# Four layers on one core: where eight of the scatters and one batch's logits stand around the start of the first mixture of experts

## The chip, the cores and the metric

The program runs on one core of a Trainium2 chip. Four layers, each an attention and a mixture or feed-forward part, are one launch. The metric is the device time of that launch in microseconds (us). The engines that matter here are TensorE (PE), VectorE (DVE), ScalarE (ACT), GpSimd (POOL), which also issues the indirect DMAs, and SyncE (SP), which issues the plain ones.

## The reference

The input is x of 8 x 256 tokens with 256 channels. The change lies between the attention and the mixture of the first layer, so only that is shown. What the attention computes does not matter for the change beyond that it handles the 8 sequences one after the other.

```python
x = x + _L0_attn_ref(_layernorm(x), ...)          # causal, 16 heads of 16
x = x + _L0_ffn_ref(_layernorm(x), ...)

def _L0_ffn_ref(x, w_gate, w_shared_up, w_shared_down, w_up, w_down):
    TOPK, CAP, E = 6, 128, 64
    x_flat = x.reshape(-1, C)                      # 2048 tokens
    y_s, g_s = jnp.split(x_flat @ w_shared_up, 2, axis=-1)
    shared = jax.nn.silu(g_s) * y_s @ w_shared_down
    scores = jax.nn.sigmoid(x_flat @ w_gate)
    _, topk_idx = jax.lax.top_k(scores, TOPK)
    w = ...                                        # the six scores, made to sum to 1
    # place of a token in its expert's list: how many earlier tokens chose that expert
    x_disp = zeros((E, CAP, C)).at[flat_e, pos].set(x_flat[token_ids], mode='drop')
    h_r = silu(g_r) * v_r                          # up product of each expert, split in two
    out_r = jnp.einsum('ech,ehd->ecd', h_r, w_down)
    routed = (y_ts.reshape(N, TOPK, C) * w[:, :, None]).sum(axis=1)
    return shared + routed
```

## The kernel before

**Stages.** Each stage is a block of its own (`with nc.Block()`), with one instruction stream for each engine. A block ends with a drain of each engine and a barrier, then POOL clears the stage's semaphores, then comes a second barrier (class `Stage`, lines 64 and 65). So an instruction of the mixture's stage starts only when all engines have ended the attention's. The attention's block is opened in line 1103, the mixture's in line 1813.

**Batches and quads.** The 2048 tokens are 16 tiles of 128, and a batch is one sequence, thus two tiles (QT = 2). The attention runs 32 quads (`QUADS`), four for each batch. The routing of a batch for the mixture is woven into the quads that come after its attention: class `Places`, with the steps statistics, normalised rows, transposes ("turned"), logits and choice, ranks, gates, and sending. `EARLY = 6`: batches 0 to 5 are routed in the quads, batches 6 and 7 at the start of the mixture's stage.

**Scatters.** A routed token is sent to its six experts. For one tile and one of the six choices, POOL issues one indirect DMA that writes 128 rows of 336 floats to the table `places` in HBM (`send`, line 1540). That is 12 scatters for a batch and 96 in all. Batches 0 to 4 are sent by `pool_end` in the quads, three scatters a quad. Batch 5 gets its gates in the last quad, and `pool_end` sends the first `in_front` of its 12 scatters there, behind POOL's four small operations (`rstd`) for batch 6. They are the last instructions of POOL in the attention. The rest of batch 5 is sent by POOL's program of the mixture's stage, which first runs `rstd` for batch 7, then sends what is left of batch 5, then waits for the gates of batch 6 (`row_ready`) and sends its 12, and the same for batch 7. One semaphore, `places.sent`, counts all 96.

**The loop over the experts.** SP waits for all 96 scatters and then loads the row tile of one expert after another (line 1823). PE transposes it, multiplies it up, transposes the hidden tile and multiplies it down, ACT and DVE do the activation, the product and the copies, and POOL adds the product to the sums with an indirect DMA (line 2020). Nothing of the loop can start before the last scatter has landed.

**PE at the start of the mixture's stage.** With `first` = batch 6 and `second` = batch 7, PE runs in the order written in the program: `turn(first)` (four transposes of the normalised rows into bank 4, line 1572), `shared_up(0)` (the shared expert's up products of the first 512 tokens, 8 instructions in the trace, line 1842), `logits(first)` (line 1579), `turn(second)`, `ranks(first)` (lines 1586 and 1587), `logits(second)`, and then the rest of the shared expert. `logits` waits until ACT has copied the transposes of its batch (`places.copied`, line 1906). `shared_up(0)` waits for the copies of batches 0 and 1, which were made in the attention. DVE takes the logits of batch 6 through `read_logits`, `pick` and `choose`, then PE makes the ranks, and DVE goes on with `read_ranks`, `place`, `weigh` and `gates` (the last, line 1712, writes the gates into the rows and releases POOL).

Of the kernel before, what the change touches and what calls it, by code (L numbers as in the profile page):

```python
# [43 lines left out]
def need(eng, sem, value):  # L44

    if isinstance(value, int) and value <= 0:
        return
    eng.wait_ge(sem, value)
# [1407 lines left out]
class Places:  # L1456
# [4 lines left out]
    FIRST, PER_BATCH, EARLY = 7, 4, 6  # L1461
    STATS, NORMED, TURNED, CHOSEN, RANKED, GATED, SENT = 0, 1, 2, 2, 3, 4, 5
    SETUP = 7
    in_front = 4

    def __init__(self, core, cfg, scratch, stack, router_in, earlier_in, base_in, token_in, shared_in):
        nc, E = core.nc, cfg.E
# [280 lines left out]
def fixed_experts_stage(core, cfg, places, up_in, down_in):  # L1748
# [15 lines left out]
    def steps_of(enter, up, turn, leave):  # L1764

        for n in range(E + 3):
            for work, at in ((enter, n), (up, n - 1), (turn, n - 2), (leave, n - 3)):
                if work and 0 <= at < E:
                    work(at)
# [13 lines left out]
    def logits_of(b):  # L1783
        return route_bank[b][:, 0:QT * E]

    def ranks_of(b):
        return route_bank[b][:, 256:256 + QT * E]

    with Stage(core) as st:
# [23 lines left out]
        with nc.Block() as block:  # L1813

            @block.sync
            def _(sp):
                sp.dma_start(up_w[:], up_in).then_inc(weights_loaded, 16)
                sp.dma_start(down_w[:], down_in).then_inc(weights_loaded, 16)
                sp.wait_ge(places.sent, 16 * TILES * TOP)
                for e in range(E):  # L1820
                    if e >= RING:
                        sp.wait_ge(added[(e - RING) % SUMS], landed(e - RING))
                    sp.dma_start(tile_rows[e % RING][:], scratch.rows[e * ROOM:e * ROOM + P, :]).then_inc(row_loaded[e % RING], 16)
                for r in range(SUMS):
                    sp.wait_ge(added[r], landed(E - SUMS + r))
                    for n in range(PARTS):
                        sp.dma_start(part_of(results[r], n), part_of(scratch.sums[r][0:TILES * P, :].rearrange("(p t) c -> p t c", p=P), n))\
                            .then_inc(results_loaded[r][n], 16)

            @block.tensor  # L1830
            def _(pe):
                def turn(b):
                    places.transposes(pe, b, [turn_bank[b][:, n * P:(n + 1) * P] for n in range(QT * KT)]).then_inc(places.turned, 1)

                def shared_up(c):
                    tokens = slice(c * CHUNK, (c + 1) * CHUNK)
                    pe.wait_ge(places.copied, (c + 1) * (B // CHUNKS))
                    need(pe, shared_added, 2 * (c - 1))
                    for u, (to, done) in enumerate(zip(shared_bank[c % 2], (s_gate_done, s_up_done))):
                        for kt in range(KT):  # L1840
                            at = (u * KT + kt) * SH
                            ins = nc.tensor.matmul(to[0:SH, :], shared[:, at:at + SH], norm_t[:, kt, tokens], start=(kt == 0), stop=(kt == KT - 1))
                        ins.then_inc(done, 1)

                def shared_down(c):
                    pe.wait_ge(s_hidden_ready, c + 1)
                    for j in range(TC // 2):
                        for t in (2 * j, 2 * j + 1):
                            ins = nc.tensor.matmul(shared_bank[c % 2][j][:, (t % 2) * C:(t % 2 + 1) * C], s_hidden[c % 2][:, t * P:(t + 1) * P],
                                                   shared[0:SH, 2 * KT * SH:2 * KT * SH + C], start=True, stop=True)  # L1850
                        ins.then_inc(s_y_done, 1)

                def transpose_rows(e):
                    pe.wait_ge(row_loaded[e % RING], 16 * (e // RING + 1))
                    need(pe, x_t_copied, e - 1)
                    for kt in range(KT):
                        ins = nc.tensor.transpose(x_bank[e % 2][:, kt * P:(kt + 1) * P], tile_rows[e % RING][:, kt * P:(kt + 1) * P], core.ident[:])
                    ins.then_inc(x_t_done, 1)

                def up(e):  # L1860
                    if e == 0:
                        pe.wait_ge(shared_added, 2 * CHUNKS)
                        pe.wait_ge(weights_loaded, 32)
                    pe.wait_ge(x_t_copied, e + 1)
                    need(pe, hidden_ready, e)
                    for kt in range(KT):
                        ins = nc.tensor.matmul(up_bank[:, 0:2 * H], x_t[e % 2][:, kt, :], up_w[:, e, kt, :], start=(kt == 0), stop=(kt == KT - 1))
                    ins.then_inc(up_done, 1)

                def transpose_hidden(e):  # L1870
                    if e == 0:
                        pe.wait_ge(zeroed, 1)
                    pe.wait_ge(hidden_ready, e + 1)
                    need(pe, h_copied, e)
                    nc.tensor.transpose(h_bank[:, 0:P], hidden[e % 2][:], core.ident[:]).then_inc(h_done, 1)

                def down(e):
                    pe.wait_ge(h_copied, e + 1)
                    need(pe, product_ready, e - 1)
                    at = slice(e % PACK * H, e % PACK * H + H)  # L1880
                    nc.tensor.matmul(y_bank[e % 2][:, 0:C], hidden_t[e % 2][at, :], down_w[at, e // PACK, :], start=True, stop=True).then_inc(y_done, 1)

                first, second = LAST
                pe.wait_ge(places.loaded, 16 * len(places.early_loads))
                turn(first)
                shared_up(0)
                places.logits(pe, first, logits_of(first))
                turn(second)
                places.ranks(pe, first, ranks_of(first))
                places.logits(pe, second, logits_of(second))  # L1890
                shared_up(1)
                shared_down(0)
                places.ranks(pe, second, ranks_of(second))
                shared_up(2)
                shared_down(1)
                shared_up(3)
                shared_down(2)
                shared_down(3)
                steps_of(transpose_rows, up, transpose_hidden, down)
# [1909 lines left out]
```

## Time and profile before

| what | us |
|---|---|
| median of 3 runs | 2983.94 |
| their range | 2980.67 to 2985.32 |
| the profiled execution, its own time | 2979.16 |
| span of the profiled execution | 2977.4 |
| granted TensorE clock, mean over the span | 0.921 |
| the attention's last instructions end (PE, POOL, DVE) | 249.4, 248.9, 250.1 |
| first instruction of the mixture's stage (SP) | 255.07 |
| last of the 96 scatters ends | 299.62 |
| first load of the loop over the experts | 301.23 |

Times in the rows count from the start of the span. The profiled execution took 1.76 us more than its span. It is shorter than each of the three timed runs; the four together average 2982.3.

In a timeline a row is: start, length, engine, line, operation, output and input tiles, how many were merged, and in brackets how long the engine had been idle and what ended that. PEld is PE's weight load. A name with a q (POOLq, DVEq) is the sequencer of the engine, which runs drains and semaphore instructions. These are in the trace, but don't count as busy time. The granted clock (PEclk) is 0.50 at 1.2 GHz and 1.00 at 2.4 GHz.

### The profile page before, as it was taken

Reading aid. Unit: us, or ns where it says so; the run is one execution under the profiler, and the core shown is the slowest. Engines: PE = TensorE matmul, PEld = TensorE weight load, DVE = VectorE, ACT = ScalarE, POOL = GpSimd, SP = SyncE. Lnnn points to the kernel's source line nnn. Section 1 sums busy time; section 2 is a strip of 40 time slices with the busy share of each in tenths; the row PEclk is TensorE's granted clock in tenths of the full one; section 3 lists DMA queues with packets and bytes.
Section 4 is the critical chain, followed back from the end, with each engine's and each line's share of the span. In section 5 each row is a group of like instructions: output and inputs, shape, how many; then the busy total and the mean of one; then the engine's idle time right before and its main releaser. Section 6 shows DMA issues by size and latency. Waiting matters only on the chain. (4 is left out here: it accounts for less than half of the span.)

```text
span 2977.4 us, 64818 instructions
## 1 busy us (share of the span) xinstructions
PE 2598.9 (87%) x19777; PEld 2191.0 (74%) x19777; DVE 1950.5 (66%) x6166; ACT 1522.3 (51%) x4590; POOL 950.7 (32%) x884
## 2 busy tenths in 40 slices
PE   6886995899986799999967499999999998799996
PEld 4663663666654699999946389999999988467774
DVE  5785334777875788788853567777777788344554
ACT  5872222899985555555553344444444444123332
POOL 3366453211003322222225411111111155436664
PEclk8998555999998899999989799999999999899998
DMA  8324565999201201010024433333333233846677
GB/s 293 88 85 190 111 113 137 346 371 346 78 2 46 78 29 54 30 61 29 29 96 154 158 103 102 92 96 102 102 95 93 86 131 132 331 102 114 116 117 160
DMA packets 260129, 371.94 MB, mean 125 GB/s; under 512 B 32112, under 2 KB 226088, under 8 KB 256912
## 3 DMA queue, kind: packets, MB, share of 16 engines
q1 hardware_dynamic: 219344, 301.42, 31.6%
q0 software_dynamic: 40512, 67.14, 11.1%
q8 instruction: 139, 2.28, 0.3%
q14 instruction: 134, 1.10, 0.1%
HBM read 109.03 MB, written 175.55 MB: 96 GB/s over the span
## 5 line engine op out<-in xcount | busy, mean ns | idle before, releaser
L671 PE MATMUL bank<-norm_t_high,w 128*128 128x256 f32 (+1 forms) x2176 | 446.9, 287 | 8.5 <-DVE w L870 8.5
L835 ACT ACTIVATE probs<-bank,neg_max 128x256 f32<-128x256 f32 (+1 forms) x512 | 224.5, 443 | 404.0 <-DVE inv L951 395.8
L1279 ACT ACTIVATE probs<-neg_scores,bound 128x256 f32<-128x256 f32 (+1 forms) x768 | 367.2, 486 | 23.5 <-DVE bound L1358 22.5
L671 PEld LDWEIGHTS bank<-norm_t_high,w 128*128 128x128 f32 x2176 | 363.4, 194 | 9.1 <-issue 9.1
L671 PE MATMUL bank<-norm_t_low,w 128*128 128x256 f32 (+1 forms) x1088 | 310.2, 285 | 0.0
L1358 DVE CUSTOM_DVE_ANT_0 neg_scores<-bank,table 128x256 f32<-128x256 f32 (+1 forms) x768 | 262.2, 396 | 52.3 <-PE bank L1189 52.3
L986 POOL TENSOR_TENSOR summed<-turned 128x512 f32<-128x512 f32 x64 | 82.4, 1288 | 612.8 <-DVE turned L902 603.0
L3269 POOL DMA_INDIRECT sums<-norm_ffn x127 | 197.3, 1553 | 156.1 <-ACT norm_ffn L3166 120.6
L731 PE MATMUL bank<-k,q 128*128 128x256 f32 (+1 forms) x1536 | 245.2, 296 | 0.0
L957 DVE SCALAR_TENSOR_TENSOR x_sb<-bank,inv,x_sb 128x256 f32<-128x256 f32 (+1 forms) x512 | 224.3, 480 | 29.3 <-DVE inv L951 19.2
L843 ACT ACTIVATE probs_t<-bank 128x384 fp32r<-128x384 f32 (+1 forms) x256 | 139.4, 545 | 202.5 <-PE bank L741 202.3
L671 PE MATMUL bank<-w,out_t 128*128 128x256 f32 x1536 | 229.1, 285 | 10.2 <-DVE out_t L943 10.2
L758 PE MATMUL bank<-probs_t,v 128*128 128x256 f32 (+1 forms) x1536 | 218.2, 278 | 3.3 <-issue 2.2
L671 PEld LDWEIGHTS bank<-w,out_t 128*128 128x128 f32 x1536 | 201.6, 190 | 13.9 <-DVE out_t L943 11.5
L671 PEld LDWEIGHTS bank<-norm_t_low,w 128*128 128x128 f32 x1088 | 211.0, 194 | 0.0
L1203 PE MATMUL bank<-ident_sb,probs 128*128 128x128 f32 x1408 | 194.8, 279 | 15.6 <-ACT probs_t L1286 15.6
L731 PEld LDWEIGHTS bank<-k,q 128*128 128x128 f32 x1536 | 197.2, 191 | 10.2 <-issue 0.2
L758 PEld LDWEIGHTS bank<-probs_t,v 128*128 128x128 f32 x1536 | 199.4, 190 | 5.3 <-DVE probs_t L938 2.4
L1203 PEld LDWEIGHTS bank<-ident_sb,probs 128*128 128x128 f32 x1408 | 155.4, 142 | 60.8 <-issue 30.7
L3118 PE MATMUL bank<-weights,shared 128*128 x508 | 174.5, 467 | 0.7 <-DVE shared L3228 0.3
L1403 POOL TENSOR_SCALAR k_placed<-k_t,place 128x512 f32<-128x512 f32 x48 | 74.4, 1565 | 305.4 <-ACT k_t L1253 305.4
L938 DVE TENSOR_TENSOR probs_t<-bank,probs_t 128x384 fp32r<-128x384 f32 (+1 forms) x256 | 158.2, 618 | 16.2 <-ACT probs_t L843 14.9
(426 smaller groups left out, 6003.0 us busy)
## 6 DMA issues: line engine op xcount, KB each, us to landing
rows<-blank SPq DMA_DIRECT2D x1, 77976.0 KB, 241.4
z<-norm_t_high SPq DMA_DIRECT2D x96, 256.0 KB, 2.5
z<-norm_t_low SPq DMA_DIRECT2D x96, 256.0 KB, 2.5
norm_ffn<-rows SPq DMA_DIRECT2D x127, 152.0 KB, 2.6
weights<-in_experts SPq DMA_DIRECT2D x1, 17024.0 KB, 49.9
q_turned<-halves SPq DMA_DIRECT2D x256, 64.0 KB, 2.0
k_turned<-halves SPq DMA_DIRECT2D x256, 64.0 KB, 2.0
places<-blank_wide SPq DMA_DIRECT2D x1, 10752.0 KB, 33.2
```

The lines of the kernel that those rows point to most:

```text
L671: ins = nc.tensor.matmul(out, stationary(a), moving(c), start=(kt == 0 and m == 0), stop=(kt == n - 1 and m == 2))
L731: ins = nc.tensor.matmul(s[:, score_columns(causal, t)], qq[a][:, j, t * P:(t + 1) * P], kk[c][:, kj, 0:width], start=False, stop=(n == 2 ...
L758: ins = nc.tensor.matmul(o_bank[:, to], vv[a][:, kt, jv * P:(jv + 1) * P], pp[c][:, of], start=(kt == 0 and n == 0), stop=(kt == QT - 1 an ...
L835: ins = nc.scalar.activation(probs[j % 2][:, t, 0:width], s_bank[j % 2][:, score_columns(causal, t)], ACT.Exp, bias=neg_max[j % 2][:, t:t ...
L843: nc.scalar.activation(probs_t[j % 2][0][:], t_bank[:, 0:NB], ACT.Copy).then_inc(t_high, 1)
L938: nc.vector.tensor_tensor(probs_t[j % 2][1][:], t_bank[:, 0:NB], probs_t[j % 2][0][:].bitcast(F32), ALU.subtract).then_inc(t_low, 1)
L957: ins = nc.vector.scalar_tensor_tensor(tile, y_bank[j % 2][:, t * C:(t + 1) * C], inv[j % 2][:, t:t + 1], tile, ALU.mult, ALU.add)
L1203: ins = nc.tensor.transpose(t_bank[g % 2][:, at:at + P], probs[q % 2][g][:, t, kt * P:(kt + 1) * P], core.ident[:])
L1279: ins = nc.scalar.activation(probs[q % 2][g][:, t, 0:width], neg_scores[g][:, t, 0:width], ACT.Exp, bias=bound[q % 2][:, g, t:t + 1], scal ...
L1358: ins = nc.vector.tensor_tensor_reduce(out=neg_scores[g][:, t, 0:width], in0=s_bank[g][:, t * S:t * S + width], in1=table[:, at:at + width ...
L3118: ins = nc.tensor.matmul(up_bank[e % 2][:, 0:COLUMNS], x_t[e % 2][:, kt, :], weights[:, kt * COLUMNS:][:, bass.ds(expert[e], COLUMNS)], st ...
L3269: nc.gpsimd.indirect_dma_start(scratch.results[e % SUMS], bass.IndirectOffsetOnAxis(ids, 0), product[e % OUT_RING], None, compute_op=ALU.a ...
```

## The change

Two edits, both around the border between the attention's block and the mixture's. `in_front` goes from 4 to 8: POOL issues eight scatters of batch 5 behind its last `rstd` in the attention, and four fewer in the mixture's stage. And on PE, `logits(first)` stands in front of `shared_up(0)` rather than behind it.

```diff
 class Places:
     FIRST, PER_BATCH, EARLY = 7, 4, 6
     STATS, NORMED, TURNED, CHOSEN, RANKED, GATED, SENT = 0, 1, 2, 2, 3, 4, 5
     SETUP = 7
-    in_front = 4
+    in_front = 8
...
                 turn(first)
+                places.logits(pe, first, logits_of(first))
                 shared_up(0)
-                places.logits(pe, first, logits_of(first))
                 turn(second)
                 places.ranks(pe, first, ranks_of(first))
                 places.logits(pe, second, logits_of(second))
```

On PE, at the start of the mixture's stage: `bank4<-ident_sb,rows_9` is `turn(first)`, `bank2<-router_w_11,norm_ffn_8` is `logits(first)`, the two rows into bank 0 and bank 1 are `shared_up(0)`, `bank5` is `turn(second)`, and the last row begins `ranks(first)`. The order counts a matmul once where the trace has two records of it.

```order
 L1572 MATMUL bank4<-ident_sb,rows_9 128x128 x4
+L1579 MATMUL bank2<-router_w_11,norm_ffn_8 128x64 x4
 L1842 MATMUL bank0<-norm_ffn_8,shared_10 64x512 x2
 L1842 MATMUL bank1<-norm_ffn_8,shared_10 64x512 x2
-L1579 MATMUL bank2<-router_w_11,norm_ffn_8 128x64 x4
 L1572 MATMUL bank5<-ident_sb,rows_9 128x128 x4
 L1586 MATMUL bank2<-chosen_bf_18,earlier_bf_15 128x128
```

The four matmuls of the logits have moved up past the four of the shared product, and nothing else on PE moved.

On POOL, at the end of the attention's block (the branch of line 1103 leaves it, the instruction of line 64 is the clearing of the semaphores):

```order
 L1533 TENSOR_TENSOR shift<-meanvar,rstd 128x2
 L1535 TENSOR_SCALAR shift<-shift 128x2
-L1540 DMA places_0<-rows_9,slot_28 131072x336 x4
+L1540 DMA places_0<-rows_9,slot_28 131072x336 x8
 L1103 UNCONDITIONAL_BRANCH
 L64 ISA
```

Four more scatters now stand ahead of the block's end. In the mixture's stage 28 follow the `rstd` of batch 7, where 32 did; the instructions of DVE, ACT and SP are the same in both programs.

## Rows read from the trace of the kernel before

**Rows 1.** The page: the span, and the chain that ended last.

```profile
span 2977.4 us, 64818 instructions
PE bank L3118 5%; PE bank L3135 4%; PE bank L3107 1%; PE bank L3126 1%; PE bank L3084 1%; PE bank L3095 1%; DMA rows<-rows,slot 1%; DMA weights<-sums 0%; DMA shared<-in_shared 0%; DMA sums<-norm_ffn 0%; DMA norm_ffn<-rows 0%; DVE x_sb L3258
```

**Rows 2.** Line 1103 (attention's end), 248 to 258 us: ns min/median/max, first and last start.

```profile
L1103 POOLq DRAIN  x1: 10563/10563/10563, 243.7 to 243.7; - x1
L1103 PEldq DRAIN  x1: 3337/3337/3337, 246.1 to 246.1; - x1
L1103 DVEq DRAIN  x1: 723/723/723, 249.4 to 249.4; - x1
```

**Rows 3.** Timeline of POOL around the border of the two stages.

```profile
247.97 0.96 POOL L1540 DMA_INDIRECT places<-rows,slot  x1 [0.30 <-issue]
...
258.04 1.07 POOL L1540 DMA_INDIRECT places<-rows,slot  x1 [0.17 <-issue]
...
269.58 0.96 POOL L1540 DMA_INDIRECT places<-rows,slot  x1 [1.53 <-DVE rows L1712]
...
298.66 0.96 POOL L1540 DMA_INDIRECT places<-rows,slot  x1 [0.30 <-issue]
```

**Rows 4.** The same drain of POOL at the ends of two other stages.

```profile
L611 POOLq DRAIN  x1: 12966/12966/12966, 2530.5 to 2530.5; - x1
L1103 POOLq DRAIN  x1: 6296/6296/6296, 823.8 to 823.8; - x1
```

**Rows 5.** Timeline of POOL: its last instruction in those two stages.

```profile
2537.10 0.96 POOL L2771 DMA_INDIRECT rows<-rows,slot  x1 [0.30 <-issue]
823.81 6.18 POOL L1403 TENSOR_SCALAR k_placed<-k_t,place 128x512 f32<-128x512 f32 x4 [38.02 <-ACT k_t L1253]
```

**Rows 6.** Stretches of the span: length, busy us by engine, PEclk, DMA share, GB/s.

```profile
250.00:254.00 4.00, 0.00 (x0) 0.00 (x0) 0.11 (x1) 0.00 (x0) 0.00 (x0) 0.93 0.00 0
...
259.00:260.00 1.00, 1.00 (x3) 0.36 (x2) 0.00 (x0) 0.00 (x0) 0.69 (x2) 0.50 1.23 524
260.00:261.00 1.00, 1.00 (x3) 0.27 (x2) 0.00 (x0) 0.00 (x0) 0.70 (x2) 0.87 1.22 524
```

**Rows 7.** Timeline of all engines from the start of the mixture's stage.

```profile
255.27 1.09 PE L1572 MATMUL bank<-ident_sb,rows 128*128 128x128 f32 x4 [5.88 <-PEq L65]
256.29 5.60 PE L1842 MATMUL bank<-norm_ffn,shared 128*64 128x512 f32 x8
256.39 0.60 ACT L1906 ACTIVATE norm_ffn<-bank 128x512 f32<-128x512 f32 x1 [11.37 <-PE bank L1572]
...
258.90 0.23 PEld L1842 LDWEIGHTS bank<-norm_ffn,shared 128*64 128x64 f32 x1 [0.63 <-issue]
259.76 0.23 PEld L1842 LDWEIGHTS bank<-norm_ffn,shared 128*64 128x64 f32 x1 [0.63 <-issue]
260.44 0.14 PEld L1842 LDWEIGHTS bank<-norm_ffn,shared 128*64 128x64 f32 x1 [0.45 <-issue]
260.87 0.14 PEld L1842 LDWEIGHTS bank<-norm_ffn,shared 128*64 128x64 f32 x1 [0.29 <-issue]
261.82 1.10 PE L1579 MATMUL bank<-router_w,norm_ffn 128*128 128x64 f32 x8
262.76 0.61 PE L1572 MATMUL bank<-ident_sb,rows 128*128 128x128 f32 x4
262.96 0.29 DVE L1654 COPY padded<-bank 128x128 f32<-128x128 f32 x1 [6.53 <-PE bank L1579]
265.47 0.23 PE L1586 MATMUL bank<-chosen_bf,earlier_bf 128*128 128x128 bf16 x1 [2.10 <-DVE seen L1675]
...
269.01 0.29 DVE L1712 TENSOR_TENSOR rows<-exps,inv 128x128 f32<-128x128 f32 x1
```

**Rows 8.** Timeline of DVE and of SP's queue, up to the loop.

```profile
295.91 0.69 DVE L1950 TENSOR_TENSOR x_sb<-bank,x_sb 128x512 f32<-128x512 f32 x1 [0.17 <-PE bank L1849]
301.23 96.34 SPq L1823 DMA_DIRECT2D tile_rows<-places  x39
```

## The prediction

> **What bounds the kernel now.** The page gives the size of the whole [rows 1]; its chain of what ended last is followed back through the last layer only, so it says nothing of the first mixture, where the change lies. There I read the timeline at both sides of the border between attention and mixture, and the records of the sequencers.
>
> The mixture's side first. The loop over the experts starts when the last of the 96 scatters has landed. POOL issues them one behind the other: from 269.58 to 298.66 there are 24, so one takes (298.66 - 269.58) / 23 = 1.264 us, of which 0.96 is in the record [rows 3]. SP's first load follows at 301.23 [rows 8]. The shared product is done before that: DVE's last addition starts at 295.91 and takes 0.69, which ends 3.0 us ahead of the last scatter (298.66 + 0.96 = 299.62) [rows 3, 8]. So POOL's scatters are the path. They were held up once in this stage: POOL waited 1.53 us until DVE had written the gates of batch 6, and went on at 269.58 [rows 3]. At this place the two things that the change touches meet. Behind it stand the 24 scatters of batches 6 and 7, and the change leaves them as they are. The time is therefore start of the stage + way to the gates of batch 6 + 24 scatters.
>
> Then the attention's side. PE's drain ends at 246.1 + 3.34 = 249.4 and DVE's at 249.4 + 0.72 = 250.1, but POOL's began at 243.7 and lasted 10.56, until 254.26 [rows 2]. POOL's last scatter had ended at 247.97 + 0.96 = 248.93 [rows 3]. The drain held 5.33 us longer, and it is what ended the block: PE's first instruction of the next stage starts at 255.27 [rows 7]. A look at POOL's busy time alone would call it free from 248.93 on and put the end at DVE's 250.1. The drain says that it is the last.
>
> **The change part by part.**
>
> Four more scatters in the attention. They stand behind the last `rstd`, directly ahead of the drain. 4 x 1.264 = 5.06 us, so the last ends at 253.99. The question is what the drain then does. At the end of the last layer's attention, six scatters end at 2537.10 + 0.96 = 2538.06 and the drain at 2530.5 + 12.97 = 2543.47, thus 5.41 later; where POOL's last work is no DMA, it ends at 823.81 + 6.18 = 829.99 and the drain at 823.8 + 6.30 = 830.10, thus 0.1 later [rows 4, 5]. So 5.3 to 5.4 us is a price that follows the last scatter, be it behind four or six of them, and not a fixed point of time. The block then ends at 254.26 + 5.06. The cover that hid nothing before hides nothing now. I take +5.06 for the start of the mixture's stage, with 0 below (if the 5.33 us are slack in which four scatters fit). All engines start later by that.
>
> Four fewer scatters in the mixture's stage. POOL starts its first one 258.04 - 255.27 = 2.77 behind PE's start [rows 3, 7]. It now has 4 rather than 8 to issue before batch 6 and is free at (on the old clock of the stage) 258.04 + 4 x 1.264 = 263.1. That would be worth 5.06 if nothing else came. But the gates of batch 6 were ready only at 269.01 + 0.29 = 269.30 [rows 7], after all eight scatters. The saving is swallowed by the wait: with the gates unmoved POOL still goes on at 269.58, and the wait grows from 1.53 by the time of four scatters, to 6.6 us. Worth 0, except as far as the gates come earlier.
>
> Logits ahead of the shared product. This is what moves the gates. On the old clock of the stage: the transposes end at 256.36, the copy on ACT ends at 256.39 + 0.60 = 256.99 [rows 7], and the logits can start at some 257.03; PE is idle 0.7 us there, where before it went straight into the shared product, which does not need this copy. The logits took 1.10 us at the high clock [rows 7]; now they run at 1.2 GHz, since the granted clock was 0.50 in 259 to 260 and rose within 260 to 261 [rows 6]. The transposes took 1.09 at the low clock and 0.61 at the high one [rows 7], a factor of 1.8, so I take 2.0 us for the logits (between 1.1 and 2.2): they end at 259.0. DVE needed from 262.96 to 265.47 for read, pick and choose, 2.51 us [rows 7], and is ready for the ranks at 261.6. But PE is not. Between them stand now `shared_up(0)` and `turn(second)`. An instruction of the shared product took 259.76 - 258.90 = 0.86 at the low clock and 260.87 - 260.44 = 0.43 at the high one [rows 7]. The 0.87 of 260 to 261 puts the rise at 260.26 [rows 6]. From 259.0 to there 1.5 of the 8 are done, the other 6.5 take 2.8, until 263.1, and the transposes 0.6, until 263.7. So the ranks start at 263.7 rather than 265.47: 1.8 us earlier, bounded by PE and no longer by DVE. The gates follow by the same DVE work, 1.8 earlier. Logits at the high clock's pace give 2.2; a rise 1.7 later gives about 0.9.
>
> PE's side afterwards: the wait for the ranks is gone, so the rest of the shared product comes no later within the stage. It starts 5.06 later in all, and what waits for the last addition would see it at 296.6 + 5.1 = 301.7 at most, while PE's first work of the loop comes after SP's first load at 301.2 + 3.3 = 304.5 [rows 8]. Covered, with 2.8 us left. SP's loads of the experts' weights (6.3 MB by the tiles' sizes) also start with the block, 5.06 later; at the 524 GB/s of 259 to 260 [rows 6] they take some 12 us, and are in place 30 us before the loop.
>
> The sum: 5.06 (the block ends later) + 0 (four fewer, swallowed) - 1.8 (gates of batch 6 earlier) = +3.3 us. Nothing behind it is changed: 24 scatters, landing, loop, three layers. Of the profiled execution that makes 2979.16 + 3.3 = 2982.5. That execution is faster than each of the timed runs; the four average 2982.3, which gives 2985.6, and the median gives 2987.2. I take **2986**, which is +0.11%, inside the 0.2% (6.0 us) that a measurement of this kernel can tell from no change.
>
> A rule of the skill, against a row. In the trace no DMA moves any byte from 250 to 254, while the drain still holds [rows 6]. By the Trainium skill, DMA: Bandwidth & Descriptors, section "Anatomy of one DMA — SWDGE (gpsimd) path", a DMA issued by GpSimd has a fixed cost of about 2.0 us plus bytes over 436 GB/s. If the drain waited for just that, the estimate from this page for one scatter (128 rows of 336 floats, 0.17 MB) would be 2.4 us, and the drain would have ended at 251.3; the row has 254.26, so the measurement decides. The four scatters would by that page end the new block at 256.4, +2.1 rather than +5.06.
>
> **The rivals.**
>
> B, the drain's time is slack. If the 5.33 us behind the last scatter run out from something earlier than that scatter, some of the four fit in. At the far end the stage starts where it did and only the swap counts: 0 - 1.8 = -1.8 us, 2980.5 by the average; halfway (2.5 - 1.8) it is +0.7, 2983. For it: DMA traffic had ended by 250 and PE and DVE too, so nothing visible is worked on [rows 2, 6]. Against it: the tail was the same in two stages of quite different ends, and nearly nothing without scatters [rows 4, 5]. The rule of the Trainium skill above would put it at 2.1 - 1.8 = +0.3, near the middle of this case.
>
> C, the swap brings nothing. The order on PE changes, but the gates don't come earlier, since PE's idle 0.7 us and the logits at 1.2 GHz eat it, or since the ranks are held by something that I don't see. Then the full +5.06 stays: 2987.4 by the average. For it: PE's rows say that it is busy without a gap from 256.29 to 263.4 [rows 7], and the swap adds work at the low clock to that. Against it: 2.1 us of idle on PE ahead of the ranks is there to be taken [rows 7]. This is also the case in which the change doesn't do what it says.
>
> D, slower. The mechanism is the clock at `shared_up(0)`, which now stands between the logits and the ranks. PE starts after 11 us of idle, rather than 5.9, and has a new gap of 0.7 us in its first 2 us. If the clock then stays at 1.2 GHz until the shared product is through, that takes 8 x 0.86 = 6.9, from 259.2 to 266.1, and the transposes 1.1: the ranks start at 267.2 rather than 265.47, and the gates are 1.7 later rather than 1.8 earlier. 5.06 + 1.7 = +6.8, 2989.1 by the average, +0.23%. It decides from the point where the rise comes later than some 264 on the old clock, 3.7 us behind that of before (then the ranks are where they were). Against it: PE is busy from 257.03 on nearly without a break.
>
> **How the numbers follow.** Forecast (+2.5 to +4.3): 0.61. B: 0.14, about half of it around its middle. C: 0.13. D: 0.08. The rest, 0.04, is for what I don't see, on either side. Timed runs differ by some 2 us each way, so the forecast and C reach beyond 6 us now and then, C more often: slower by over 0.2% is D's larger part (0.06), from C 0.05, from the forecast 0.05 and of the rest 0.02, which makes 0.18. Faster by over 0.2% needs -6: B at its end with the runs against it, 0.03, and 0.02 of the rest, 0.05. Within 0.2% remains 0.77. The range: below it reaches into B (2980.5) and above to D (2989) with 2 to 3 us for the runs, 2980 to 2992.
>
> **What would show it.** In the changed kernel's trace: eight scatters behind `rstd` in the attention, the last ending at some 254.0. The drain of POOL in line 1103 ending at 259.3 (B: before 258), and PE's first instruction of the stage at 260.3. Logits from 262.1 to 264.1, the ranks at 268.8 (C: 270.5; D: 272.3). POOL's wait for the gates of batch 6 at 4.8 us rather than 1.53, and the 24 scatters from 272.9 at 1.264 each. SP's first load at 304.5. Wrong would be the forecast if the drain's tail shrinks as scatters are added, if the rise of the clock falls elsewhere by over 2 us, or if the stages behind the loop move against each other.

## The result

The changed kernel takes 2990.41 us (median of 11 runs) against 2985.32 for the kernel before (also 11, measured beside it). Two of the 11 before were slow ones (3352.30 and 4206.07 us) and are left out of the ratio, so it is not that of the two medians. The ratio is 1.0025, with a 95% interval of 1.0013 to 1.0036: slower by some 7.5 us, between 3.9 and 10.7. The forecast was +3.3 us, inside the 0.2% that can't be told from no change. The time lies in the range, but the measured ratio is above the 0.2% that was called most likely, though its interval begins below it.

The profiled execution of the changed kernel has a span of 2995.9, 18.5 more than before. That is no measure of the change: at 2997.73 us it is the second longest of its kernel's 11 runs, and of the 18.5 us 2.7 had come about ahead of the first changed instruction and 10.2 behind the loop's first load, in code that is the same. The two profiles are therefore compared over one **stretch**, from the start of POOL's last `rstd` operation in the attention (line 1535, the last instruction ahead of the scatters in front) to SP's first load of the loop over the experts (line 1823). All that the change touches lies in it. Before it is 301.23 - 243.71 = 57.5 us, after it 309.54 - 246.37 = 63.2, thus +5.65.

Timeline of POOL in the changed kernel (start, length, engine, line, operation, tiles, idle time before and what ended it); it answers to [rows 3]:

```profile
246.37 0.19 POOL L1535 TENSOR_SCALAR shift<-shift 128x2 f32<-128x2 f32 x1
246.73 1.07 POOL L1540 DMA_INDIRECT places<-rows,slot  x1 [0.17 <-issue]
...
255.70 0.96 POOL L1540 DMA_INDIRECT places<-rows,slot  x1 [0.30 <-issue]
...
270.01 0.96 POOL L1540 DMA_INDIRECT places<-rows,slot  x1 [0.30 <-issue]
277.83 0.96 POOL L1540 DMA_INDIRECT places<-rows,slot  x1 [6.86 <-DVE rows L1712]
...
306.97 0.96 POOL L1540 DMA_INDIRECT places<-rows,slot  x1 [0.30 <-issue]
```

The drains at the end of its attention (ns min/median/max, first and last start), which answer to [rows 2]:

```profile
L1103 POOLq DRAIN  x1: 15958/15958/15958, 246.3 to 246.3; - x1
L1103 DVEq DRAIN  x1: 725/725/725, 252.2 to 252.2; - x1
```

The timeline of SP's queue, which answers to [rows 8]:

```profile
263.14 0.34 SPq L1817 DMA_DIRECT2D up_w<-in_up  x1
...
309.54 20.01 SPq L1823 DMA_DIRECT2D tile_rows<-places  x11
```

POOL's eighth scatter ends at 256.66, DVE is done at 252.9, and POOL's drain holds the block until 246.3 + 15.96 = 262.3. In the mixture's stage POOL sends its four, then waits 6.86 us for the gates of batch 6, where it had waited 1.53.

All engines from the start of the mixture's stage, which answers to [rows 7]:

```profile
263.33 1.09 PE L1572 MATMUL bank<-ident_sb,rows 128*128 128x128 f32 x4 [11.16 <-PEq L65]
264.46 0.60 ACT L1906 ACTIVATE norm_ffn<-bank 128x512 f32<-128x512 f32 x1 [16.77 <-PE bank L1572]
265.11 1.97 PE L1579 MATMUL bank<-router_w,norm_ffn 128*128 128x64 f32 x8 [0.69 <-ACT norm_ffn L1906]
...
267.00 6.30 PE L1842 MATMUL bank<-norm_ffn,shared 128*64 128x512 f32 x8
267.11 0.29 DVE L1654 COPY padded<-bank 128x128 f32<-128x128 f32 x1 [2.62 <-PE bank L1579]
...
269.09 0.49 DVE L1675 TENSOR_TENSOR seen<-seen,chosen 128x64 bf16<-128x64 bf16 x2
...
273.24 0.66 PE L1572 MATMUL bank<-ident_sb,rows 128*128 128x128 f32 x4
...
273.73 0.22 PE L1586 MATMUL bank<-chosen_bf,earlier_bf 128*128 128x128 bf16 x1
```

And the granted clock there (stretch, its length, busy us of PE, PEld, DVE, ACT and POOL, the clock, DMA share and GB/s), which answers to [rows 6]:

```profile
271.00:272.00 1.00, 1.00 (x2) 0.23 (x1) 0.00 (x0) 0.00 (x0) 0.00 (x0) 0.50 1.37 589
272.00:273.00 1.00, 1.00 (x3) 0.23 (x1) 0.00 (x0) 0.00 (x0) 0.00 (x0) 0.81 1.36 578
```

DVE has the choice of batch 6 ready at 269.6. PE gets to the ranks at 273.73, since `shared_up(0)` stands between and runs at 1.2 GHz until 272.4. So the 5.65 us are made up as follows, each taken as a difference of two starts. The mixture's stage starts (SP, line 1817) 16.77 us behind the last `rstd` operation rather than 11.36: +5.41. From there POOL's first scatter of batch 6 comes after 14.69 us rather than 14.51: +0.18. The 24 scatters and the landing take 0.06 more.

### The profile page after: what moved, and what is told of

The parts are those of the page before. It is cut to its first block and busy times, and to the rows that moved or that the text cites. A ratio compares the mean times of both kernels' runs of the same rounds, so it can differ in the third digit from the quotient of the medians.

```text
span 2995.9 us, 64818 instructions
## 1 busy us (share of the span) xinstructions
PE 2607.7 (87%) x19777; PEld 2197.6 (73%) x19777; DVE 1949.8 (65%) x6166; ACT 1524.1 (51%) x4590; POOL 952.5 (32%) x884
## 5 line engine op out<-in xcount | busy, mean ns | idle before, releaser
L1279 ACT ACTIVATE probs<-neg_scores,bound 128x256 f32<-128x256 f32 (+1 forms) x768 | 366.9, 485 | 24.5 <-DVE bound L1358 23.6
L1358 DVE CUSTOM_DVE_ANT_0 neg_scores<-bank,table 128x256 f32<-128x256 f32 (+1 forms) x768 | 262.0, 396 | 56.7 <-PE bank L1189 56.7
```

The source lines that it names most:

```text
L1279: ins = nc.scalar.activation(probs[q % 2][g][:, t, 0:width], neg_scores[g][:, t, 0:width], ACT.Exp, bias=bound[q % 2][:, g, t:t + 1], scal ...
L1358: ins = nc.vector.tensor_tensor_reduce(out=neg_scores[g][:, t, 0:width], in0=s_bank[g][:, t * S:t * S + width], in1=table[:, at:at + width ...
```

## The experiments

Two theories were open. **T**: each scatter in front of the drain costs its time in full, since POOL's drain ends the block a fixed time behind POOL's last instruction. **K**: the swap's gain is real but is lost in the shared product, which PE runs at the low clock. Their rivals: that the swap itself did the harm, that the drain's time can hold other work, and that the late clock was chance.

The table has for each run: scatters in front; POOL's drain, from the end of POOL's last operation; start of the mixture's stage from the start of the last `rstd` operation; rise of the clock to 2.4 GHz and start of the ranks of batch 6, both from PE's first instruction of the stage (the rise read from stretches of a quarter us); the stretch; and, where it was timed, the ratio to the kernel before with its interval. "High" means that the stage began at the high clock and fell from it or kept it. The drain's start stands in the lines to a tenth of a us; the table takes it to the hundredth from the traces, and so differs by up to 0.05 from the 4.95, 5.33 and 5.60 of the expectations.

| run | in front | drain | stage start | rise | ranks | stretch | ratio |
|---|---|---|---|---|---|---|---|
| before | 4 | 5.30 | 11.36 | 5.0 | 10.20 | 57.5 | |
| changed | 8 | 5.63 | 16.77 | 9.1 | 10.40 | 63.2 | 1.0025 (1.0013 to 1.0036) |
| e1_scatters_only | 8 | 5.63 | 16.76 | 6.1 | 10.78 | 63.5 | 1.0020 (1.0008 to 1.0032) |
| e2_swap_only | 4 | 5.31 | 11.37 | 7.8 | 9.77 | 57.1 | 1.0000 (0.9987 to 1.0012) |
| e3_front0 | 0 | 4.99 | 7.11 | high | 7.93 | 57.0 | 1.0007 (0.9996 to 1.0018) |
| e4_front12 | 12 | 5.96 | 22.15 | 4.3 | 9.83 | 68.7 | |
| e5_swap_front6 | 6 | 5.47 | 14.08 | 6.7 | 9.23 | 59.3 | |
| e6_pe_kept_busy | 8 | 5.63 | 16.74 | high, fell | 9.31 | 62.0 | 1.0019 (1.0003 to 1.0035) |
| e7_front2 | 2 | 5.14 | 8.68 | high, fell | 9.43 | 56.7 | 1.0004 (0.9989 to 1.0018) |
| e8_narrow_ahead | 4 | 5.30 | 11.38 | 8.9 | 13.83 | 61.2 | |
| e9_shared_behind | 8 | 5.63 | 16.75 | 12.0 | 6.30 | 59.1 | 1.0011 (1.0002 to 1.0020) |
| e10_ahead_of_rstd | 2 | 5.14 | 8.67 | high, fell | 9.65 | 55.2 | 1.0002 (0.9990 to 1.0014) |
| e11_memsets_behind | 4 | 5.32 | 15.38 | 3.7 | 9.54 | 61.1 | |
| e12_before_again | 4 | 5.30 | 11.37 | 5.5 | 10.49 | 57.9 | 1.0001 (0.9986 to 1.0016) |

The runs e5 to e8, e11 and e12 were made on chips on which the kernel before takes 3068 to 3070 us rather than 2983 to 2985; each ratio is to the kernel before on the same chip.

**One edit at a time.** e1 and e2 take the two edits apart.

```diff
-    in_front = 4
+    in_front = 8
```

> Only in_front 8, the order on PE as before. I measure the stretch from POOL's last rstd operation in the attention (line 1535) to SP's first load of the loop (line 1823): 57.5 us before, 63.1 in the changed kernel. Theory (a scatter ahead of the drain costs its full time, the drain ends 5.3 to 5.6 us behind the last one, and the wait for the gates swallows what is saved later): block end 5.1 to 5.3 later within the stretch, stretch 62.6 to 62.9, and POOL waits some 6.6 us for the gates of batch 6. Rival (the swap is what costs, the scatters fit in partly): stretch 60 or less. Timed: about +5 us, ratio 1.0017.

```diff
                 turn(first)
+                places.logits(pe, first, logits_of(first))
                 shared_up(0)
-                places.logits(pe, first, logits_of(first))
```

> Only the swap on PE, in_front 4 as before. Theory (the swap gains up to 1.8 us when the clock rises as in the kernel before, and nothing or a little loss when it rises late; which of the two is chance): stretch between 55.7 and 57.7, ranks 8.4 to 10.4 us behind PE's start of the stage (10.2 before, 10.4 in the changed kernel). Rival (the swap always delays the rise of the clock): rise about 8.9 us behind PE's start as in the changed kernel, ranks at 10.4, stretch 57.7. Timed: within 0.1% of before.

The scatters alone give a stretch of 63.5 and a ratio of 1.0020, the swap alone 57.1 and 1.0000. The loss is that of the scatters. With the swap alone the stretch is 0.4 us shorter than before (57.5; 57.9 in e12), with a rise of the clock at 7.8. Theory and rival of e2 both allowed for such a stretch, so e2 doesn't decide between them; e5 and e8 below bear on it. What I expected of e1 held but for 0.6 us: POOL's wait was 7.25 rather than 6.6, with the ranks at 10.78.

**How many scatters.** e3, e4, e5 and e7 change only the number: the diff is that of e3, and e4 has 12 in its place, e7 has 2, and e5 is the changed kernel, with the swap, and 6.

```diff
-    in_front = 4
+    in_front = 0
```

> in_front 0, the order on PE as before: no scatter stands behind the last rstd. Theory (the drain ends 5.3 us behind the last scatter, whatever stands between): POOL's last scatter is that of the last quad, so the drain ends before DVE is through, the block ends by DVE and the mixture's stage starts some 4 us earlier; POOL then has 12 scatters ahead of the gates of batch 6 and is the later one, so of the 4 us only about 0.5 is left: stretch 57.0. Rival (the drain's 5.3 us are paid at the block's end whatever POOL did last): block end 5.3 us behind the last rstd operation, no earlier start than 1.3 to 3 us, stretch 58 to 60.

> in_front 12, the order on PE as before: all of batch 5 ahead of the drain. Theory: linear, 8 x 1.264 = 10.1 us later than before, drain's end again 5.3 to 5.6 behind the last scatter, POOL waits some 11.6 us for the gates of batch 6, stretch 67.6 to 68.1. Rival (the time behind the last scatter grows with each scatter, as 5.33 with four and 5.60 with eight may be read): 5.9 or more with twelve, stretch 68.2 or more.

> in_front 2, the order on PE as before. Theory: the stage starts at 11.36 - 2 x 1.35 = 8.7 behind the last rstd operation, POOL is bound by its own scatters (ten of batch 5 in the stage, the gates are ready before they are through), stretch 55.9 to 56.3, 1.2 to 1.6 us under the kernel before. Rival (the drain has a fixed part that shows with any scatter behind rstd): start at 10 or later, stretch 57.5. Timed: within 0.1% of before, too little to be told by the clock of the device; the stretch decides.

The start of the stage is at 8.7, 11.4, 14.1, 16.8 and 22.2 for 2, 4, 6, 8 and 12: 1.35 us for each, of which 1.265 is the scatter and 0.083 a longer drain. With none it is 7.1, and there the block ended by DVE: POOL's drain ended at 249.0, DVE's at 250.1. Here the expectation was wrong in one point. Drains of e3, the second one that of DVE:

```profile
L1103 POOLq DRAIN  x1: 5060/5060/5060, 243.9 to 243.9; - x1
L1103 DVEq DRAIN  x1: 725/725/725, 249.4 to 249.4; - x1
```

POOL's last scatter had ended at 242.25 and its last `rstd` operation at 244.01. The drain did not end 5.3 behind the scatter but 6.75, which is 4.99 behind the `rstd` operation. e11 below is about that. The stretch of e3, 57.0, came as expected: 4.25 us earlier start, and POOL with its 12 scatters of batch 5 then later than the gates. e4 shows the other end. Its drain of POOL:

```profile
L1103 POOLq DRAIN  x1: 21065/21065/21065, 243.8 to 243.8; - x1
```

And POOL's wait for the gates of batch 6 in e4, in the timeline:

```profile
280.34 1.07 POOL L1540 DMA_INDIRECT places<-rows,slot  x1 [11.59 <-DVE rows L1712]
```

With no scatter of batch 5 left in the stage, POOL waits 11.59 us there, and the stretch is 68.7, above the 67.6 to 68.1 of the theory and at what the rival said: the time behind the last scatter does grow, by 0.083 us for each scatter, to 5.96. e7 was 0.4 us longer than expected. One of its scatters started 1.76 us behind the one before rather than 1.27, which is all of it; I have no cause for that.

**What the drain waits for.** e11 puts other work behind the scatters.

```diff
                     dispatch.pool_end(pool, q, ...)
+                for n in range(4):
+                    pool.wait_ge(zeroed, 2 + n)
+                    nc.gpsimd.memset(windows[0][:].rearrange("p t h w -> p (t h w)"), 0.0).then_inc(zeroed, 1)
```

> The kernel before (in_front 4), with four memsets of a tile that nobody reads any more behind POOL's last scatter of the attention, 0.95 us each and some 4 us in all. Theory S (the 5.3 us of the drain run from the last scatter on, whatever POOL does in them): the memsets fit in, drain's end 5.3 to 5.5 behind the last scatter, start of the stage 11.4 to 11.6 behind the last rstd operation, stretch as before. Rival O (the drain pays about 5 us behind POOL's last operation once scatters have gone ahead; for it speaks that with in_front 0 the drain ended 4.95 behind the last rstd operation and 6.71 behind the last scatter): drain's end 9 us or more behind the last scatter, start at 15 or later, stretch 61 or more. In between (7 to 8 us behind the last scatter) would say that a part of it runs on beside other work.

Timeline of POOL in e11, and then its drain:

```profile
272.80 0.96 POOL L1543 DMA_INDIRECT places<-rows,slot  x1 [0.30 <-issue]
273.76 3.99 POOL L1421 MEMSET windows<- 128x1024 f32 x4
```

```profile
L1103 POOLq DRAIN  x1: 6288/6288/6288, 276.8 to 276.8; - x1
```

The memsets end at 277.75 and the drain at 283.07: 5.32 behind the memsets, 9.31 behind the last scatter. The rival O was right: the drain's time runs from POOL's last instruction, whatever that is.

This is not the completion of the scatters. SP's first load waits for all 96 of them, and in all fourteen traces it starts 1.6 us behind the end of the last one's record (before: 299.62 and 301.23), while in e11 the drain ended 9.31 us behind the last scatter. By the Trainium skill, DMA: Bandwidth & Descriptors, section "Anatomy of one DMA — SWDGE (gpsimd) path", a DMA issued by GpSimd has a fixed cost of about 2.0 us. The trace is near that: the load comes 2.57 us behind the start of the last scatter.

The traces also show what sets the length. The attention's block has 60 scatters of batches 0 to 4 and those in front, and the drain ends 4.99, 5.14, 5.30, 5.47, 5.63 and 5.96 us behind POOL's last instruction with 60, 62, 64, 66, 68 and 72 of them: 0.083 us for each indirect DMA of the whole block. Two other blocks of the kernel before bear this out. The last layer's attention has 66 and 5.46 us (the prediction's 5.41, which was read from tenths) [rows 4, 5]. The block of line 2234 has 32 + 47 = 79; the last of them ends at 1663.35, POOL's last addition at 1680.43 and the drain at 1686.97, thus 6.54 behind the addition, again 0.083 for each, although no indirect DMA had been issued for 23.6 us. POOL there (the groups with counts, two rows of the timeline, and the drain):

```profile
L2594 POOL DMA_INDIRECT products<-shared,norm_t x47 | 45.1, 959 | 36.1 <-ACT shared L2405 35.5 <-issue 0.6
L2587 POOL DMA_INDIRECT rows<-token_rows,slot x32 | 30.9, 965 | 33.6 <-ACT token_rows L2375 24.2 <-issue 9.4
```

```profile
1662.39 0.96 POOL L2594 DMA_INDIRECT products<-shared,norm_t  x1 [0.30 <-issue]
...
1671.97 8.46 POOL L2600 TENSOR_TENSOR x_sb<-x_sb,weights 128x1024 f32<-128x1024 f32 x3 [0.63 <-DMA weights<-products]
```

```profile
L2234 POOLq DRAIN  x1: 10041/10041/10041, 1676.9 to 1676.9; - x1
```

In a block without indirect DMAs the drain ends 0.1 behind the last instruction [rows 4, 5]. The count does not give the length in the two blocks with a loop over experts, whose last indirect DMAs add to the sums: 96 with 6.6 us and 157 with 3.8. So the 0.083 is read from these three blocks, and no run set out to test it. What the drain does in this time the traces don't say.

**The clock.** e5 is one more case with the swap, and e8 takes the gap on PE and the late shared product apart.

> The changed kernel with in_front 6. So far the mixture's stage starts 7.1, 11.4, 16.8 and 22.2 us behind POOL's last rstd operation with 0, 4, 8 and 12 scatters in front. Theory (each one costs 1.35 us, of which 1.264 is its own): start at 14.1. And on the clock, theory A (it rises 3.2 to 5.4 us behind the first instruction of the shared product, which the swap puts 3.7 rather than 1.0 behind PE's start): rise 6.9 to 9.1 behind PE's start, ranks at 9.3 to 10.4, stretch to SP's first load 59.8 to 60.7. Rival (the late rise in the two kernels with the swap is chance): a rise as in those without it, 4.2 to 6.2, ranks at 8.0 to 9.0, stretch down to 58.4.

```diff
                 turn(first)
+                for _ in range(2):        # batch 5's logits, into a part of a bank that is overwritten later
+                    for t in range(QT):
+                        for kt in range(KT):
+                            nc.tensor.matmul(route_bank[second][:, t * E:(t + 1) * E], ...)
                 shared_up(0)
```

> The kernel before, but PE makes batch 5's logits twice more, into a part of a bank that is overwritten later, between the transposes of batch 6 and the shared product. So the narrow matmuls stand ahead of the shared product as in the changed kernel, but PE has no gap in front of them. Added work: 16 records of 0.24 us, 3.8 us on PE. Theory A (what counts is how late the shared product starts): first shared instruction 4.8 us behind PE's start, rise 8.0 to 10.2 behind PE's start. Rival G (it is the gap of 0.7 us that put the rise off): rise 4.2 to 6.2 behind PE's start as in the kernels without the swap. Stretch longer than 57.5 by 2 to 4 us in either case, from the added work.

PE in e8 from the start of the stage, and then the stretch in which its clock rises:

```profile
277.85 1.09 PE L1572 MATMUL bank<-ident_sb,rows 128*128 128x128 f32 x4 [4.68 <-PEq L65]
278.73 3.52 PE L1889 MATMUL bank<-router_w,norm_ffn 128*128 128x64 f32 x16
282.17 5.93 PE L1842 MATMUL bank<-norm_ffn,shared 128*64 128x512 f32 x8
```

```profile
286.00:287.00 1.00, 1.00 (x2) 0.23 (x1) 0.00 (x0) 0.00 (x0) 0.76 (x1) 0.60 0.15 65
```

PE is busy without a gap from 277.85 on, and the clock was granted in full only from 286.8 on, 8.9 behind PE's start but 4.6 behind the first instruction of the shared product. So it is not the gap of 0.7 us. Over the ten kernels of the table in which PE starts the stage at the low clock the rise comes 3.7 to 12.0 us behind PE's start, but 2.7 to 5.4 behind the start of `shared_up(0)` (before: 255.27 + 4.98 - 256.29 = 4.0, after: 263.33 + 9.05 - 267.00 = 5.4). e5 lies at 3.0, just below the 3.2 that I had given as the lower end; its ranks (9.23) and stretch (59.3) also lie just under what theory A gave and above what its rival gave. The swap puts the start of the shared product from 1.0 to 3.7 behind PE's start, and the rise goes with it. With the swap the ranks then come at 10.40, 9.77 and 9.23, without it at 10.20, 10.78, 9.83, 10.49 and 9.54: on the mean 9.80 against 10.17. That is 0.4 us in favour of the swap, but cases of the same order differ by over 1 us by where the rise falls, so that it can't be told from nothing.

**Giving PE the high clock, or nothing to run between.** e6 keeps PE busy over POOL's drain; e9 moves the shared product away.

```diff
                 for kind in ("inv", "spread", "y"):
                     product(kind, B - 1)
+                if dispatch:
+                    pe.wait_ge(bound_ready, 4 * QUADS)
+                    for n in range(9):        # nobody reads the result
+                        nc.tensor.matmul(s_bank[0][:], out_t[:, 0, 0:P], wo[:]..., start=True, stop=True)
```

> The changed kernel, and at the end of PE's program in the attention nine matmuls of 512 columns whose result nobody reads; they run while POOL still sends and drains, so that PE comes to the mixture's stage without the long idle time. Theory (the swap's gain was lost to the low clock): the clock is high when the stage starts, the ranks come 6.5 to 7 us behind PE's start rather than 10.4, POOL's wait for the gates shrinks from 6.9 to some 3.3, and the stretch from 63.2 to some 59.5; the start of the stage stays at 16.8 behind the last rstd operation, since PE is done before POOL. Rival (the clock has no part in it, or the ranks wait for something else on PE): ranks at 9.5 or later, stretch 62 or more. Timed: some 3.5 us less than the changed kernel, still 2 us over the kernel before.

```diff
                 places.logits(pe, first, logits_of(first))
-                shared_up(0)
                 turn(second)
                 places.ranks(pe, first, ranks_of(first))
+                shared_up(0)
                 places.logits(pe, second, logits_of(second))
```

> The changed kernel (in_front 8, logits of batch 6 first), and shared_up(0) moved on behind the ranks of batch 6, so that nothing of the shared product stands between that batch's logits and its ranks. Theory (the swap's gain is lost in the shared product, which PE runs at the low clock while DVE's choice is ready): the ranks start about 6.3 us behind PE's start, when DVE is ready, rather than 10.4; POOL's wait for the gates shrinks from 6.9 to some 2.5; its 24 scatters start 10.5 us behind the stage's start, stretch 58.7 to 59.3, start of the stage unmoved at 16.8. Rival (the ranks wait for something else, DVE or the transposes of batch 7): ranks at 9 or later, stretch 62 or more. Timed: some 4 us less than the changed kernel, still 1 to 2 over the kernel before.

e6 missed. Its granted clock over the start of the stage:

```profile
285.00:286.00 1.00, 0.00 (x0) 0.00 (x0) 0.00 (x0) 0.00 (x0) 0.00 (x0) 1.00 0.00 0
286.00:287.00 1.00, 0.56 (x4) 0.46 (x4) 0.71 (x2) 0.00 (x0) 0.00 (x0) 0.87 0.00 0
287.00:288.00 1.00, 0.31 (x3) 0.05 (x1) 0.57 (x5) 0.60 (x1) 0.42 (x2) 0.50 1.56 459
...
293.00:294.00 1.00, 1.00 (x3) 0.36 (x2) 0.00 (x0) 0.00 (x0) 0.90 (x1) 0.72 0.15 66
```

The stage began at the high clock, but PE had been idle from 284.34 to 286.44, and the clock fell at 286.7 and was back at 293.6. The ranks came at 9.31, where 6.5 to 7 was expected. So e6 settles nothing about what a high clock would give to the swapped order, and no other run does. For the old order e3 has it: the clock was high from PE's start until behind the ranks, and these came at 7.93 rather than 10.20. e9 does settle what stands in the way of the ranks. PE in e9:

```profile
265.99 1.11 PE L1572 MATMUL bank<-ident_sb,rows 128*128 128x128 f32 x4
...
268.51 0.29 PE L1586 MATMUL bank<-chosen_bf,earlier_bf 128*128 128x128 bf16 x1 [1.41 <-DVE seen L1675]
...
268.84 6.28 PE L1842 MATMUL bank<-norm_ffn,shared 128*64 128x512 f32 x8
```

The ranks come at 6.30, when DVE is ready, POOL's wait shrinks from 6.86 to 2.90 (2.5 was expected) and the stretch from 63.2 to 59.1, as expected. It is still 1.6 us over the kernel before (ratio 1.0011), since the start of the stage is where eight scatters put it.

**A shorter row of scatters.** By T few scatters in front are best, and POOL's own row is then the path. e10 also fills POOL's wait for DVE's statistics.

```diff
-    in_front = 4
+    in_front = 2
...
+                ahead = 2
+                for n in range(places.in_front, places.in_front + ahead):
+                    places.send(pool, places.EARLY - 1, n)
                 places.rstd(pool, B - 1)
                 for b in range(places.EARLY - 1, B):
                     pool.wait_ge(places.row_ready, b + 1)
-                    for n in range(places.in_front if b == places.EARLY - 1 else 0, QT * TOP):
+                    for n in range(places.in_front + ahead if b == places.EARLY - 1 else 0, QT * TOP):
```

> in_front 2, the order on PE as before, and in the mixture's stage POOL sends two scatters of batch 5 ahead of the rstd of batch 7, in the time in which it waits for DVE's statistics. Theory (POOL's row of scatters is the path from the stage's start on, so 1.2 us of its idle time go): start of the stage 8.7 behind the last rstd operation, no wait for gates, last scatter's start 44.1 to 44.3 behind the stage's start rather than 45.4, stretch 55.3 to 55.6, about 2 us under the kernel before. Rival (batch 7's rows come later by the later rstd, and hold PE and thereby the ranks of batch 6 up): POOL waits for the gates, stretch 57 or more. Timed: 0.05 to 0.1% under the kernel before, which five rounds will hardly tell from nothing.

The stretch is 55.2, 2.3 under the kernel before and a little better than expected, and POOL waits for no gates. The ratio of 1.0002 (0.9990 to 1.0014) can't tell 2 us from nothing, so this is no proven gain for the whole.

**The control.**

> The kernel before once more, unchanged, as a control: it gives a second profile of it with its own state of the clock, and says what a ratio of 1 looks like. Theory: ratio 1.000 with an interval of 0.0012 to either side, rise of the clock 4.2 to 6.2 behind PE's start, ranks at 9.8 to 10.8, stretch 57.2 to 58.0. Were the ratio 1.0005, the 1 to 2 us by which most timed ratios of this study exceed what the stretch shows would be an offset of the comparison; were the stretch 59 or more, the one profile of before would have been a lucky one.

The kernel before against itself gives 1.0001 (0.9986 to 1.0016), and its second profile a stretch of 57.9. So the profile of before was an ordinary one. The timed differences of this study are by 0 to 3 us larger than those of the stretches (7.5 against 5.65 for the changed kernel). Their intervals hold the smaller numbers in each case, and the control gives no offset; whether something behind the loop has a part in it stays open.

## Why the prediction was wrong

The larger term and its sign were right: the drain had been seen as what ends the block, and the four scatters as not hidden. +5.06 was forecast for the start of the stage, +5.41 measured; the 0.35 more is the drain's own growth (4 x 0.083 = 0.33). That it is a price "that follows the last scatter", the same "be it behind four or six of them", was wrong: e11 shows that it follows POOL's last instruction of any kind, and it grows with all the scatters of the block. The two tails that I compared stand behind 64 and 66 scatters, not four and six. For this change that was worth only the 0.33. Rival B, that the drain's time is slack, fell: neither scatters nor memsets fitted into it.

Four fewer scatters in the stage were costed at 0, since the wait for the gates would swallow them; the wait grew to 6.86, where 6.6 stood for unmoved gates. Right.

The step that failed is the swap, the term of -1.8. It measured +0.18 in the profiled kernel, and -0.4, within the scatter of the cases, by the mean of the ranks over three with it and five without. Its first half held: the logits took 1.97 us where 2.0 was taken, DVE was ready for the ranks 6.2 us behind PE's start (269.58 - 263.33), where 6.3 was forecast. What failed is "the 0.87 of 260 to 261 puts the rise at 260.26": I took the time of the rise from the order before and left it standing on the clock of the stage, 5.0 us behind PE's start. It goes with the shared product, which the swap itself had put off by 2.7 us. At 9.05 instead of 4.98, more than six of the eight records (272.38 - 267.00 over 0.86 us) ran at the low pace before the ranks, rather than the 1.5 of the sum. The text had the point from which it turns, "later than some 264 on the old clock" or 8.7 behind PE's start; the rise at 9.05 was just past it, and the swap gave just nothing. With the rise as measured the prediction's own working gives the ranks of all three kernels with the swap: 0.86 us for each record of the shared product up to the rise, 0.43 behind it and 0.6 for the transposes make 10.40, 9.76 and 9.22 for the changed kernel, e2 and e5, where 10.40, 9.77 and 9.23 were measured. So the working was sound and the time of the rise was not. So D's mechanism was the true one in the middle of its range, without D's full price, and the result in the stretch, +5.65, is C's number (+5.06) by D's way. I had given the two 0.21 together and dismissed D since "PE is busy from 257.03 on nearly without a break", which e8 shows to be no reason.

The sum with the right terms, 5.4 + 0.2, is +5.65 us or 0.19%, at the edge of what counts as a change. The measured 1.0025 is on the other side of that edge, and its interval reaches from 0.13% to 0.36%. The chance of 0.77 for "within 0.2%" was too high for a forecast whose own unfavourable end lay at 0.23%.

## What to carry to other kernels

The end of a block is set by the last drain, and POOL's drain can be the last while its busy time ends long before. In the attention's block here it ended 0.083 us for each of the block's 60 to 72 indirect DMAs behind POOL's last instruction, and in another block the same for each of 79, though the last of them stood 17 us ahead of it. Scatters that are put at such an end cost their full time, and the same scatters in the next stage may stand in a wait that is there anyway; look for the wait first, then decide on which side of the border they belong. When instructions are swapped on TensorE after an idle time, don't leave the rise of the clock standing where it was: here it came later by about what the swap had put off the shared product. And a work item that others wait for gains only as far as what still stands between it and its reader lets it.

## What the hardware showed that I had not expected

- The drain of POOL: 4.99 us behind the last instruction with 60 scatters in the block, 5.30 with 64, 5.63 with 68, 5.96 with 72 and 6.54 with 79 indirect DMAs, also where four memsets of 1 us (5.32, e11) or 17 us without an indirect DMA stand in between. That is 0.083 us for each.
- The clock's rise: 2.7 to 5.4 us behind the first 512-column instruction in each of the ten kernels in which PE started the stage at the low clock, while transposes and 64-column matmuls ran ahead of it for 1.0 to 6.6 us. With 3.5 us of narrow matmuls without a gap in front (e8) it came at 8.9.
- A pause of 2.1 us of PE at the high clock (e6) was followed by 6.8 us at the low one, though PE worked through most of these.
- The same kernel takes some 2984 us on some chips and 3069 on two others, while the stretch studied here agrees to 0.4 us between them (57.5 and 57.9).
